# Two chunks of rows instead of one between the second layer's row pass and the next block's first row pass

## The reference, cut to what matters

```python
x = inputs.reshape(b, G, h // G, t, s)          # 1, 1, 16, 1024, 1024
wI = w + jnp.eye(w.shape[-1], dtype=w.dtype)
ret = jnp.einsum('BGMTS,GMN->BGNTS', x, wI)
hq = jnp.einsum('BGMTS,BTGIM->BGITS', x, qw1)
ret = ret + jnp.einsum('BGITS,BTGIM->BGMTS', hq, qw2)
hk = jnp.einsum('BGMTS,BSGIM->BGITS', x, kw1)
ret = ret + jnp.einsum('BGITS,BSGIM->BGMTS', hk, kw2)
ret = ret + x * qdd.transpose(0, 2, 3, 1)[:, :, :, :, None]
ret = ret + x * kdd.transpose(0, 2, 3, 1)[:, :, :, None, :]
```

## Time and profile before

| | us |
|---|---|
| median of 3 runs | 859.1 |
| lowest, highest | 857.77, 862.08 |
| the profiled execution | 858.88 |
| its span from the first to the last instruction | 857.1 |
| TensorE busy (share of the span) | 766.5 (89%) |
| DVE, POOL, ACT busy | 546.1 (64%), 513.6 (60%), 393.6 (46%) |
| mean granted TensorE clock | 0.976 |

### The profile page before, as it was taken

How to read it: one execution, slowest core, us unless ns; L and a number is a source line. 1 busy time by engine, 2 the same in 40 slices (tenths; PEclk the granted TensorE clock), 3 DMA queues, 4 the chain that set the end, 5 groups by cost and what they waited for, 6 DMA issues and landing times.

```text
span 857.1 us, 42054 instructions
## 1 busy us (share of the span) xinstructions
PE 766.5 (89%) x18464; PEld 704.4 (82%) x18464; DVE 546.1 (64%) x809; ACT 393.6 (46%) x673; POOL 513.6 (60%) x456
## 2 busy tenths in 40 slices
PE   5998899799898999797998899979998889988998
PEld 2658799699787988797987898868998779877997
DVE  3338557468474866665676675837758566665668
ACT  6224563247432583225833466325743267324640
POOL 2326577467665677555766567646776567765733
PEclk9999999999999999989999999999999999999999
DMA  9804318952568618774098723785167840985026
GB/s 190 296 3 100 93 59 309 295 185 66 200 213 296 180 25 293 232 282 101 3 333 237 265 75 131 277 277 183 44 245 257 297 110 6 341 251 184 4 116 278
DMA packets 76045, 157.09 MB, mean 183 GB/s; under 512 B 39768, under 2 KB 40792, under 8 KB 73944
## 3 DMA queue, kind: packets, MB, share of 16 engines
q1 hardware_dynamic: 75888, 154.61, 55.5%
HBM read 85.25 MB, written 69.34 MB: 180 GB/s over the span
## 4 chain that ended last, share of the span: by engine, by line
POOL 34%; PE 25%; issue 24%; DVE 7%; DMA 5%; SPq 2%; POOLq 1%; ACT 1%; DVEq 0%; ACTq 0%
POOL WA L200 19%; POOL WB L208 9%; PE PB L655 7%; PE PA L607 7%; POOL WB L200 6%; PE PA L642 5%; PE PB L624 4%; DMA X<-in_x_dram 3%; DVE OUT L524 3%; PE PB L592 3%; DVE WB L208 2%; SPq L240 1%; DVE PROD L478 1%; DMA RT<-products 1%; DVE PROD L481 1%
## 5 line engine op out<-in xcount | busy, mean ns | idle before, releaser
L524 DVE TENSOR_TENSOR OUT<-PB,X 128x512 f32<-128x512 f32 x256 | 172.4, 686 | 185.0 <-PE PB L655 141.0
L402 ACT ACTIVATE Y<-PA 128x512 f32<-128x512 f32 (+1 forms) x256 | 147.3, 634 | 306.7 <-PE PA L607 306.7
L412 ACT ACTIVATE X<-PA 64x512 f32 (+3 forms) x384 | 232.7, 606 | 118.5 <-PE PA L642 111.8
L655 PE MATMUL PB<-Y,WB 128*128 128x128 f32 x2048 | 272.6, 286 | 1.7 <-issue 1.0
L655 PEld LDWEIGHTS PB<-Y,WB 128*128 128x128 f32 x2048 | 248.8, 193 | 15.8 <-issue 6.2
L208 POOL TENSOR_TENSOR WB<-RT,mask 128x512 f32<-128x512 f32 x128 | 156.3, 1221 | 106.1 <-PE PB L655 102.6
L511 DVE TENSOR_TENSOR Y<-PB,Y 128x512 f32 (+1 forms) x256 | 164.8, 685 | 80.7 <-PE PB L624 69.5
L607 PEld LDWEIGHTS PA<-X,WA 64*64 64x64 f32 x8192 | 149.4, 145 | 78.1 <-issue 37.8
L642 PE MATMUL PA<-Y,WA 64*64 64x128 f32 x4096 | 190.9, 311 | 20.7 <-issue 14.3
L607 PE MATMUL PA<-X,WA 64*64 64x64 f32 x8192 | 170.1, 234 | 44.0 <-DMA X<-in_x_dram 25.3
L200 POOL TENSOR_TENSOR WA<-RS,mask 128x512 f32<-128x512 f32 x128 | 139.4, 1089 | 110.7 <-PE PA L642 85.4
(11 more groups left out here) (24 smaller groups left out, 62.4 us busy)
## 6 DMA issues: line engine op xcount, KB each, us to landing
X<-in_x_dram SPq DMA_DIRECT2D x128, 512.0 KB, 6.0
out_dram<-OUT SPq DMA_DIRECT2D x128, 512.0 KB, 4.5
RT<-products SPq DMA_DIRECT2D x15, 1024.0 KB
products<-PROD SPq DMA_DIRECT2D x16, 128.0 KB, 8.2
RT<-products SPq DMA_DIRECT2D x1, 768.0 KB
QP<-in_rows_dram SPq DMA_DIRECT2D x8, 80.0 KB, 3.5
RT<-in_left_dram SPq DMA_DIRECT2D x1, 384.0 KB
RT<-products SPq DMA_DIRECT2D x1, 256.0 KB
```

What stands on the lines that cost most here:

```text
L402: nc.scalar.activation(rows_of(Y, k, j)[:, :, WIDE * h:WIDE * (h + 1), :].rearrange("q a s c -> q a c s"), PA[HALVES * (j % RING) + h][:, ...
L412: nc.scalar.activation(columns_of(block_of(X, k), dst, WIDE * i + NARROW * g), by_columns(PA[HALVES * (g % RING) + i][src, :]), ACT.Copy). ...
L524: nc.vector.tensor_tensor(rows(OUT[:, o % OUT_SLOTS]), PB[g % SLOTS][:, :].rearrange("q (a c s) -> q a c s", a=FEW2, c=PAIR), rows(rows_of ...
L655: last = nc.tensor.matmul(PB[g % SLOTS][:, COLS * r:COLS * (r + 1)], WB[:, g % SLOTS, P * r:P * (r + 1)], rows_of(Y, k, t2_chunk(o))[:, (i ...
```

## The change

TensorE's row phase takes two chunks at a time: t2 of chunks 0 and 1, then t1 of chunks 0 and 1, and so on. All work is the same, and so are the orders of the other four engines and every wait's count.

```diff
@@ -32,6 +32,7 @@
 LAG = 2
+TOGETHER = 2
 QUARTERS = 4
@@ -671,11 +672,12 @@
-                for o in range(CHUNKS):
-                    for i in range(PER_CHUNK):
-                        t2(k, PER_CHUNK * o + i)
+                for o in range(0, CHUNKS, TOGETHER):
+                    for g in range(PER_CHUNK * o, PER_CHUNK * (o + TOGETHER)):
+                        t2(k, g)
                     if k < BLOCKS - 1:
-                        t1(k + 1, o)
+                        for j in range(o, o + TOGETHER):
+                            t1(k + 1, j)
```

## The result

The changed kernel takes 871.77 us (median of 4 runs, 867.01 to 873.01), beside 860.59 for the kernel before in the same measurement: a ratio of 1.0119, with a 95% interval of 1.0063 to 1.0174. In a second measurement further down it was 1.0059 (1.0010 to 1.0109), with medians of 873.33 and 863.96 us. It is slower, by 1.2% and by 0.6%; I had forecast no change, and 871.77 lies above the range of 849 to 869. A time in this document is the median of all executions of a kernel, while a ratio leaves out those more than 1.5% above its fastest one, so that the two can differ a little.

What follows compares the result with a forecast made beforehand. TensorE, busy in 89% of the span, was taken as the bound. The terms -10.4 + 1.8 + 4.5 + 2.1 + 3 gave +1.0 us on a median of 859.1, so 860 us; range 849 to 869.

Steps and rivals of the forecast that it cites:

- Changes of form: TensorE's row phase: two of four switches between t1 and t2 per chunk pair go, 0.37 us; -10.4 us.
- c6: The start of t2 on chunk 6 in TensorE's row phase, a point from which the forecast counts.
- (b): Row phase: pieces of 256 instructions arrive late; +4.5 us ahead of chunk 6, +2.1 us behind chunk 13.
- From chunk 6 to chunk 13 nothing counts: Row phase: chunk 13's load decides when its t1 starts, before and after, so nothing is saved there.
- ACT's last copies: End of row phase: ACT's copy of t1 on chunk 15 begins 0.25 us later in each block; +1.8 us.
- Rival two: Row phase: pieces of instructions are late by more, and the clock drops too; 868 us, chance 0.27.
- (c): Row phase ahead of chunk 6: longer halts bring the clock down two more times; +3 us, bounds 0 and 6.
- Rival one: Row phase: instructions come in time, so late instructions and clock drops fall away; 850.5 us, chance 0.22.
- Rival three: Row phase: chunk 13's load comes earlier, so more of the 20.7 us surfaces; 840 us, chance 0.06.

Runs made afterwards that it cites:

- one_store15: Kernel before (one chunk at a time) with the products stored after chunk 15 instead of chunk 9: 833.00 us, ratio to before 0.970.
- two_noload: Changed kernel with the loads of chunks 3 to 15 left out in all blocks but the first: 813.57 us.
- early_last: Kernel before with products computed early and stored late, plus two chunks at a time only for chunks 12 to 15: 832.06 us, 0.963 of before.
- the second trace: Changed kernel, nothing altered, run once more beside the kernel before: 873.33 us, ratio 1.0059.
- one_noload: Kernel before with the loads of chunks 3 to 15 left out in all blocks but the first: 808.66 us.

## Why the prediction was wrong

**Changes of form, -10.4 us.** The rate was right, though not by its sum: 64 records of 0.014 us are 0.90 us and not 0.93, which would make 0.40 us for two changes where a pair saved 0.36. As measured, a pair takes 5.86 us instead of 6.22 (I had 5.85), and the last stretch of a phase, from t1 on chunk 13 to s1, is 0.43 us shorter without halts in the kernels with loads left out (I had 0.37). Up to c6 the seven phases took 139.1 us where they took 139.0, and the forecast had 7.8 us saved there against 4.5 of (b) and 3 of the clock.

**From chunk 6 to chunk 13 nothing counts: right.** t1 on chunk 13 starts 30.0 us behind c6 before and 30.3 after, as a mean of seven phases (I had 29.5). The wait ahead of group 18 came as computed, for instance 2.34 us in the last row phase with t1, and the wait on chunk 13 behind it:

```profile
763.46 3.62 PE L656 MATMUL PB<-Y,WB 128*128 128x128 f32 x16 [2.34 <-DVE WB L209]
...
584.99 1.99 PE L608 MATMUL PA<-X,WA 64*64 64x64 f32 x64 [4.70 <-DMA X<-in_x_dram]
```

It stood in three phases only; in the others TensorE came later than DVE, since it had halted before. one_store15 confirmed the chain through SP, and two_noload the price of 2.3 us per phase once the cover is gone.

**ACT's last copies, +1.8.** Too high. The wait of s1's third group grew from 0.78 to 0.94 us, a row of before and one of after:

```profile
381.82 1.39 PE L624 MATMUL PB<-X,WB 64*64 64x128 f32 x32 [0.78 <-DVE Y L511]
```

```profile
286.15 1.38 PE L625 MATMUL PB<-X,WB 64*64 64x128 f32 x32 [0.94 <-DVE Y L512]
```

so some 1 us in all.

**(b) Late instructions, +6.6: the step that failed.** The mechanism was right and the place where I stopped counting was not. The halts grew by 28.1 us, and by place they are, of before and of the changed kernel:

| halts of "issue", us | before | changed | growth forecast |
|---|---|---|---|
| row phases, chunks 0 to 5 | 4.8 | 8.2 | 4.5 |
| row phases, chunks 6 to 12 | 10.6 | 23.7 | put at no cost |
| row phases, from chunk 13 | 0 | 4.6 | 2.1 |
| s1, first two groups | 0 | 5.5 | none |
| s1, later groups | 5.3 | 7.8 | none |
| s2 | 10.0 | 6.0 | none |
| up to the first row phase | 4.3 | 7.2 | none |

The seven halts to which I fitted the 4.5 us for a piece add up to 6.4 us and not 6.1, and three of them stand in t1 on chunk 6, behind c6; even so the growth ahead of c6 came near. Between chunks 6 and 13 the halts did grow, by 13.1 us, and cost next to nothing: they took up part of the wait on loads, which fell by 13.6 us. So in the row phases the sum held: -0.8 us without ACT's part, and +1.1 and -1.5 measured. The step failed because I ended the count at the end of the row phase, and put nothing but ACT's 1.8 us into the column phases. The two groups of t1 there are followed by s1: t1 on two chunks and two groups of s1 are 384 instructions and a few waits without a slow group among them. s1 halts in its first two groups in each of the kernels with a pair of t1 ahead of it, for 2.1 to 7.3 us in all, and for 0 to 0.2 us in the others. early_last shows exactly this part. The column phases took 7.8 us more, 6.6 and 5.7 of them in the two phases in which s1 halts three and four times, and 11.9 us more in the second trace. How much of the rest is the change and how much scatter stays open; and 4.7 of the profiled execution's 13.6 us lie ahead of the first changed instruction.

**Rival two**, pieces late by more, had the right side (868 us) and 0.27, but not by its mechanism: its 0.76 short pieces of 4.0 us in each of seven phases are 21 us of halts ahead of c6, where 8.2 stand.

**(c) The clock, +3: mis-sized.** The granted clock fell from 0.976 to 0.960, 14 us more lost by the same arithmetic. About 7 of them lie in the row phases, beyond my upper bound of 6, and 3.4 each in the column phases and ahead of the first row phase. I had priced two further drops ahead of chunk 6. A long halt anywhere can bring one, the column phases included, but not each does: after 2.49 us of halt four groups of t2 took 5.19 us, and after 2.41 us they took 3.90:

```profile
252.09 0.56 PE L608 MATMUL PA<-X,WA 64*64 64x64 f32 x19 [2.41 <-issue]
252.58 3.90 PE L656 MATMUL PB<-Y,WB 128*128 128x128 f32 x32
```

**Rival one**, that the instructions come in time, was refuted: the halts nearly doubled. The Trainium skill (Runtime: NRT & Kernel Launch, Instruction fetch mechanics) says that crossing a block of 256 instructions costs one step of the queue that is "mostly hidden". That differs from the traces here, where the halts on the grid were 34 us of 857 before and 62 of 871 after. **Rival three**, chunk 13's load earlier, didn't happen without moving SP's products.

## What to carry to other kernels

When a trace has halts of "issue" in a fast run of small multiplications, count the instructions between them; if they lie on a grid, what matters is the shortest time in which any one piece of the program can be used up, and an order that puts dense groups together shortens it. A slow group between two dense ones costs a change of form (0.36 us for both here) and buys time for the next piece; whether that pays depends on how busy the transfers are (-9.5 us with half of them, +22 to +25 with all). Count such a window across the end of the phase that is changed, and look first for what the long waits hang on: moving one store and one computation gained 5%, where the order of TensorE's groups had at most 2.4% to give.

## What the runs showed of the hardware that I had not expected

- Late instructions also cost the column phase, in every kernel: s2 has 9 to 19 us of issue halts with up to 4.4 us each, and leaving out the row phase's loads doesn't change that (14.3 us in one_noload). Whether the row matrices' loads delay the instructions there isn't shown.
- A late fetch of instructions costs its length and at times the clock behind it: four groups of t2 took 5.19 us instead of 3.90 after a halt of 2.49, but 3.9 after halts of 1.37 and 2.41.
- SP stands 5.88 us on the products' two transfers in the middle of the row phase, and 2.17 us on the same two behind it, in one_store15:

```profile
369.57 2.17 SPq L241 DMA_DIRECT2D products<-PROD  x2
```
